# A two-layer graph network on one core: its front stage loaded, normalized, written and ranked in another way

## The reference, cut to what matters

```
x = x + gnn0(layernorm(x), edges, edge attributes)   # attention over incoming edges, 8 heads
x = x + ffn0(layernorm(x))                           # 64 slices per head
x = x + gnn1(layernorm(x), edges)
x = x + experts(layernorm(x))                        # top 2 of 8 experts
```

## Time and profile before

| what | value |
|---|---|
| median of 3 runs | 4086.47 us (4084.59 to 4089.71) |
| span of the profiled execution | 4086.3 us |
| front stage (`sort_nodes`) | 1.1 to 236.2 us |
| `windows` (edge records put into slots) | 237 to about 345 us |
| layer 0's graph loop | about 345 to 1560 us |
| the slice network | about 1560 to 2000 us |
| layer 1's graph loop | about 2000 to 2950 us |
| experts | about 2950 us to the end |

### The profile page before, as it was taken

How to read it: one execution, slowest core, us unless ns; L and a number is a source line. 1 busy time by engine, 2 the same in 40 slices (tenths; PEclk the granted TensorE clock), 3 DMA queues, 4 the chain that set the end, 5 groups by cost and what they waited for, 6 DMA issues and landing times. The chain is left out here.

```text
span 4086.3 us, 69498 instructions
## 1 busy us (share of the span) xinstructions
PE 2989.6 (73%) x12787; PEld 2168.3 (53%) x12788; DVE 2289.9 (56%) x5023; ACT 1298.0 (32%) x5485; POOL 2301.6 (56%) x2343
## 2 busy tenths in 40 slices
PE   4623777787878887999666665665656489999998
PEld 3422444444444444667544444444444378898887
DVE  4533888888888887874355555555555611111111
ACT  1401444444444454432211111111111533333343
POOL 5156777777777773002577777777777623333332
PEclk9866999899999998998777777778777789999999
DMA  8635444344444442000244444444444756666564
GB/s 188 193 89 147 116 116 117 105 108 108 108 107 109 110 111 62 0 2 30 75 112 113 113 112 113 112 113 113 113 112 112 220 173 166 170 174 167 167 172 128
DMA packets 292188, 487.96 MB, mean 119 GB/s; under 512 B 145315, under 2 KB 193393, under 8 KB 291625
## 3 DMA queue, kind: packets, MB, share of 16 engines
q0 software_dynamic: 127312, 325.41, 32.1%
q1 hardware_dynamic: 155936, 158.55, 13.2%
q10 hardware_dynamic: 8880, 3.34, 0.4%
HBM read 430.09 MB, written 57.50 MB: 119 GB/s over the span
## 5 line engine op out<-in xcount | busy, mean ns | idle before, releaser
L902 POOL DMA_INDIRECT g_rows<-rows,g_recs x1856 | 1764.1, 950 | 628.9 <-issue 474.1
L947 PE MATMUL g_pA<-g_msg,k_ident 128*128 128x264 f32 (+1 forms) x3712 | 1150.2, 463 | 474.0 <-DVE g_pA L1141 409.4
L947 PEld LDWEIGHTS g_pA<-g_msg,k_ident 128*128 128x128 f32 x3712 | 805.4, 228 | 803.8 <-issue 659.1
L936 PE MATMUL g_pE<-g_ew,g_recT 128*128 128x512 f32 x932 | 511.8, 676 | 251.3 <-DVEq L1125 248.4
L1135 DVE TENSOR_TENSOR g_msg<-g_rows,g_pp 128x1024 f32 (+3 forms) x464 | 571.9, 1233 | 151.2 <-DVEq L84 151.1
L1985 POOL DMA_INDIRECT out<-e_ys,e_goal x102 | 160.7, 1576 | 501.8 <-issue 481.1
L936 PEld LDWEIGHTS g_pE<-g_ew,g_recT 128*128 128x128 f32 x932 | 170.0, 202 | 468.9 <-DVEq L1125 343.1
L2038 PE MATMUL e_pY<-e_w,e_hT 128*128 x1632 | 373.8, 382 | 30.3 <-issue 30.3
L1057 ACT ACTIVATE g_pp<-g_dd 128x32 f32<-128x32 f32 x464 | 95.2, 205 | 921.0 <-ACTq L84 921.0
L2027 PEld LDWEIGHTS e_pH<-e_xT,e_w 128*128 128x128 f32 x3264 | 382.9, 193 | 5.2
L2027 PE MATMUL e_pH<-e_xT,e_w 128*128 128x128 f32 x3264 | 383.2, 276 | 0.0
(11 more groups left out here) (418 smaller groups left out, 3446.2 us busy)
## 6 DMA issues: line engine op xcount, KB each, us to landing
e_w<-in_L_ffn_W SPq DMA_DIRECT2D x110, 1024.0 KB
g_rows<-rows,g_recs POOLq DMA_INDIRECT x1856
g_recs<-slots SPq DMA_DIRECT2D x468, 8.0 KB
tok<-e_xall SPq DMA_DIRECT2D x7, 910.0 KB
rows<-p_row SPq DMA_DIRECT2D x50, 119.0 KB
own<-p_row SPq DMA_DIRECT2D x50, 119.0 KB
p_x<-in_x SPq DMA_DIRECT2D x1, 5600.0 KB
own<-p_x SPq DMA_DIRECT2D x1, 5600.0 KB
```

Source lines behind the costliest of these rows:

```text
L902: pool.indirect_dma_start(out=rows[:, r, j, :], out_offset=None, in_=rows_d, in_offset=bass.IndirectOffsetOnAxis(ap=recs[:, r, 4 * j:4 * j ...
L936: last = t_.matmul(pE[:, c:c + 512], recT[:], ew[:].rearrange("p c d -> p (c d)")[:, c:c + 512], start=True, stop=True)
L947: last = t_.matmul(sums, K["ident"][:], of, start=False, stop=(j == C - 1), skip_group_check=True)
```

## The change

Nothing is changed in what is computed; the order of nodes within the last bucket of the sort may differ. Six edits, all but the last in `sort_nodes`:

1. The weights `wn` and `wx` are loaded by SP's queue ahead of x, not by ACT's. x comes in five parts of ten tiles (10240 bytes a partition each), with a semaphore for each.
2. DVE's order is by part: block numbers of ten tiles, some counts (`marks`: 0, 2, 4, 6, 4), statistics and variance of the part (`piece`), and the factors of the part before (`scaled`). The waits for the weights and for POOL's constants, and two new casts (`tri_b`, `ones_b`), now stand ahead of the first block numbers. ACT takes three square roots ahead of tile 0 and two more ahead of tiles 1 and 5's work.
3. The counting matmuls write to three PSUM banks that the row pipeline doesn't use.
4. Rows are written once, to `own0` only, by pairs of tiles (RB=6 buffers, three pairs); x's columns follow after each ten tiles, the edge records after the pair of tiles 30 and 31. All loops over tiles are unrolled.
5. 32 buckets in place of 64 (degrees of 31 and more share the last one), the one-hot matrix and its two weights in bf16, 4 pieces of 16 tiles, which alternate between two pairs of PSUM banks. `ranks` now stands after tile 39 in PE's program.
6. Layer 0's graph loop gathers the same 272 columns from `own0`, whose rows lie 2112 bytes apart, in place of `rows0` with 1088.

```diff
+DB = 32
-        J, R, RB, W, GT, PG, B = 2, 10, 5, 10, 10, 5, 2
+        J, R, RB, GT, PG, B = 2, 10, 6, 10, 5, 2
-        OHW = NT * NB
+        OHW = NT * DB
+        NG = NT // GT
+        hot = m.sb("p_hot", [P, NT, DB], BF16)
+        banks = (pX, pTt, pR)
+        pN = [banks[g % 3][0:P, 16 * (g // 3):16 * (g // 3) + GT] for g in range(NG)]
+        sides = ((pR, pTt), (pM, pX))
-        cols = [(a, min(a + 8, NT)) for a in range(0, NT, 8)]
+        cols = [(a, min(a + 16, NT)) for a in range(0, NT, 16)]
 # SP
-                for l in lanes:
-                    sp.dma_start(x[l, :, :], ...).then_inc(x_in, 16)
+                sp.dma_start(wn[:], ...).then_inc(w_in, 16)
+                sp.dma_start(wx[:, :, 0:D], ...).then_inc(w_in, 16)
+                for g in range(NG):
+                    for l in lanes:
+                        sp.dma_start(x[l, g * GT:(g + 1) * GT, :], ...).then_inc(x_in[g], 16)
-                        for l in lanes:
-                            sp.dma_start(rows0[l, bass.ds(W * u + r, 1), :]..., row[l, r % RB, :]).then_inc(row_out[r % RB], 16)
-                            sp.dma_start(own0[l, bass.ds(W * u + r, 1), 0:RW]..., row[l, r % RB, :]).then_inc(row_out[r % RB], 16)
+                for t in range(0, NT, 2):
+                    sp.wait_ge(row_ok, t + 2)
+                    j = t // 2 % (RB // 2)
+                    for l in lanes:
+                        sp.dma_start(own0[l, t:t + 2, 0:RW], row[l, 2 * j:2 * j + 2, :]).then_inc(row_out[j], 16)
+                    if t % GT == GT - 2:
+                        g = t // GT
+                        sp.wait_ge(x_in[g], 32)
+                        for l in lanes:
+                            sp.dma_start(own0[l, g * GT:(g + 1) * GT, RW:RX], x[l, g * GT:(g + 1) * GT, :]).then_inc(x_out, 16)
+                    if t == 3 * GT:
+                        sp.wait_ge(rec_made, 2)
+                        ... # the edge records, both lanes
 # DVE
+                def piece(g):
+                    dve.wait_ge(x_in[g], 32)
+                    for t in range(g * GT, (g + 1) * GT):
+                        last = norm.tile(v, t, x[:, t:t + 1, :])
+                    last.then_inc(tile_ok, 1)
+                    dve.wait_ge(tile_ok, g + 1)
+                    norm.variance(v, ch, stats, slice(g * GT, (g + 1) * GT))
-                index(0)
                 dve.wait_ge(w_in, 64)
                 dve.wait_ge(consts, 3)
+                v.tensor_copy(tri_b[:], K["tri"][0:P, 0:P])
+                v.tensor_copy(ones_b[:], K["ones"][0:P, 0:P])
+                marks = (0, 0, 2, 6, 12, 16)
+                for g in range(NG):
+                    index(g)
+                    for t in range(marks[g], marks[g + 1]):
+                        count(t)
+                    piece(g)
+                    if g:
+                        scaled(g - 1)
 # ACT
+                for g in range(3):
+                    root(g)
+                normed(0)
+                for t in range(NT):
+                    if t in (1, 5):
+                        root(3 + t // 5)
 # PE
+                project(0, 40)
                 ranks()
-                group(3, False, False)
-                group(4, False, True)
+                project(40, NT)
 # graph
-    rows_d, xk = dr[f"rows{layer}"], K["x"]
+    rows_d, xk = dr["own0" if layer == 0 else "rows1"], K["x"]
```

More of the change, by code:

```diff
@@ L487, in turned @@
[L487 to L495, removed]
-                    s.activation(row[:, r % RB, :], pH[r % 2][:, 0:RW], ACT.Copy).then_inc(row_ok, 1)
@@ L498, in group @@
-                def group(u, first, last_group):
-                    for r in range(W):
-                        if r < W - 1 or not last_group:
-                            normed(u, r + 1)
-                        turned(u, r)
-                        if r > 0:
-                            rows(u, r - 1, first and r - 1 < RB)
-                    rows(u, W - 1, False)
-                normed(0, 0)
-                paired(act, NT // W, group)
+                for g in range(3):
+                    root(g)
@@ new lines, in normed, with turned, rows @@
+                def normed(t):
+                    if t % GT == 0:
+                        act.wait_ge(rst, t // GT + 1)
+                    s.activation(xn[:, t % 2, :], x[:, t, :], ACT.Identity, bias=nbias[:, t:t + 1], scale=rstd[:, t:t + 1]).then_inc(xn_ok, 1)
+                def turned(t):
+                    act.wait_ge(t_ok, t + 1)
+                    s.activation(xnT[:, t % 2, :, :], pT[t % 2][:, :, 0:P], ACT.Copy).then_inc(xnT_ok, 1)
+                def rows(t):
+                    act.wait_ge(h_ok, t + 1)
+                    if t >= RB:
+                        act.wait_ge(row_out[t % RB // 2], 32 * (t // RB))
+                    s.activation(row[:, t % RB, :], pH[t % 2][:, 0:RW], ACT.Copy).then_inc(row_ok, 1)
@@ L515, in _, with counting @@
                 pe.wait_ge(below_ok, J)
-                for t in range(NT):
-                    for j in range(J):
-                        last = t_.matmul(pN[t // GT][:, t % GT:t % GT + 1], bl[:, j, t, :], ones[:], start=(j == 0), stop=(j == J - 1))
-                    last.then_inc(counted, 1)
+                def counting(g):
+                    if g >= 3:
+                        pe.wait_ge(idx_ok, g - 2)
+                    for t in range(g * GT, (g + 1) * GT):
+                        for j in range(J):
+                            last = t_.matmul(pN[g][:, t % GT:t % GT + 1], bl[:, j, t, :], ones[:], start=(j == 0), stop=(j == J - 1))
+                        last.then_inc(counted, 1)
+                counting(0)
                 pe.wait_ge(ablk_ok, 1)
@@ L562, in place @@
                     last.then_inc(placed, 1)
+                for g in range(1, NG):
+                    counting(g)
                 pe.wait_ge(wx_ok, 1)
-                turn(0, 0)
-                group(0, True, False)
-                group(1, False, False)
-                group(2, False, False)
+                turn(0)
+                project(0, 40)
                 ranks()
-                group(3, False, False)
-                group(4, False, True)
+                project(40, NT)
                 for g in range(NT // PG):
```

144 lines of the change are left out of this document (64 added, 80 removed).

## The result

| | median, us | lowest to highest, runs |
|---|---|---|
| before, same chip | 4085.53 | 4081.34 to 4089.71, 4 |
| after | 4011.18 | 4008.13 to 4011.93, 4 |

The account below looks back on a forecast made before the run. The front stage (235 us) was taken as bound by a chain that changes engines. Terms -22, -1.7, +6, -17.6, -11.8 and -17 brought its end from 236.2 to 172.9, 63 us: 4086.3 - 63 = 4023, range 4004 to 4048.

Parts of the forecast that it names:

- fetches land early: Rival, chance 0.20: beside smaller x packets, front-stage fetches land in 10 us; 4012, or 4004 if PE is never late.
- No wait for the weights: Front, ahead of the first block numbers: the wait costs nothing if weights land by 17; first fetch stays near 19.7.
- I go nearer to the upper end: 46.: Front: fetch 5, issued at 27.3, lands at 46 us, within 32 to 52, beside the loads of x.
- The taking of turns: Each DMA engine takes packets from its queues in turn; a fetch beside x needs some 9 us.
- Counts, -22: Front, fetches and counts: fetch 16 goes at 51.5, then POOL is unbroken; last count done at 109.5, was 131.2.
- DMA engines bind more: Rival, chance 0.22: fetches and writes slow each other, fetches at 1.75 us, counts end at 117.5; 4034.
- PE at `ranks` at 124: Front, row pipeline: tile 0 at 51, DMA engines then ACT bind, PE reaches `ranks` at about 124; net +6 us.
- VectorE's wait for the first sum, 9: Front: DVE waits for TensorE's first sum of `ranks`, 115 to 124, some 9 us.
- Rounds 6.4, first pair 0.7: Front, rounds of `ranks`: three full and a small one at the copies' pitch, 6.4 us against 24.0, so -17.6.
- Passes halve, -11.8: Front, DVE's passes after the rounds: 24.5 us, all but 0.9 halves with 1600 elements, -11.8.
- Place, the wait of 17 goes, 29.8 to the end: Front's end: PE reaches `place` at 143, the 16.97 us wait goes (-17); DVE's groups end at 172.9.
- I am wrong if that loop moves by more than 10 us.: Sign against the prediction: layer 0's loop, expected still some 1215 us, moves by more than 10 us.

Follow-up runs that it names:

- e12: Changed kernel with the loads of x's parts 2 to 4 and the edge data held behind the first two counts: 4019.08 us, ratio 0.9829.
- e4: Changed kernel with x's columns written behind all rows, not after each ten tiles: 4008.09 us, ratio 0.9795.
- e7: Changed kernel with the statistics of four parts ahead of the counts on VectorE: 4001.94 us, ratio 0.9791.
- e11: Changed kernel with the reorderings of e7 and e4 together: 3998.76 us, ratio 0.9781.
- e3: Kernel before with only the 32 buckets in bf16 and two pairs of banks, `ranks` still after tile 29: 4070.49 us, ratio 0.9951.
- e8: Changed kernel with `ranks` after tile 29 in place of tile 39: 4015.34 us, ratio 0.9823.
- e2: Kernel before with only layer 0's gathers taken from the wide table `own0`: 4088.39 us, ratio 0.9997.
- e9: Kernel before with seven more semaphore increments in the front on VectorE alone: 4063.18 us, ratio 0.9937.
- e5: Kernel before with only the bucket cap set to 31, so node order changes but no instruction is added or removed: 4087.22 us, ratio 1.0001.

## Why the prediction was right, and where it was wrong

The kernel is faster by more than the forecast said and the time lies in the range, but two errors stand against each other in it: the front gave 15 us less than forecast, later stages 29 us that it did not have. That the time came within 12 us is luck. The time is that of the rival "fetches land early" (4012), whose steps did not happen: it had the last count at 101.6 and tile 0 at 43.

- *No wait for the weights.* VectorE waited 2.5 us, for a constant of POOL, and the first fetch was at 19.8 against 19.69. Right.
- *"I go nearer to the upper end: 46."* This step failed. Fetch 5 was there for its count at 55.3 to 55.9, not 46. I took the six fetches as landing together after one latency. They came one behind another: counts at 37.1, 44.0, 49.8, 52.3, 55.3, 55.9. e12 shows the cause, the loads beside them. The taking of turns, as the prediction worked it out (one packet of q1 for each of a fetch's ten on an engine), is too cheap by far: from 19 to 37 us q1's 458 packets took 92.1% of the engines' time, 0.58 us each, so ten turns would be 5.8 us, and even with the 5.9 of a fetch alone before them 11.7, not 17.4. For each of q0's 253 packets q1 got 1.8 through; why is open. Tile 0 followed at 61.5, not 51 (+10.5).
- *Counts, -22.* Measured -7: the last one was done at 124.2. 11.1 of the 14.7 us too few are the late start (fetch 16 issued at 62.65, not 51.5). 2.1 were lost among the 33 fetches behind it, in one wait for a count (1.58 at 79.00) and one issue of 2.12 us (at 83.52); the others kept the pitch of 1.51, so "fetches stay at 1.51 us" was right, and the 1.75 of the rival "DMA engines bind more" did not come. The last 1.5 are a later landing of fetch 49 (issued at 114.58). VectorE waited 3.75, 3.23, 3.60 and 3.42 us for fetches (at 96.7, 100.6, 116.2 and 120.3), 10 to 14 us after x's columns had been issued, but these waits held up no later fetch. In e4 and e7 the last count was late behind its fetch where a big write stood beside it, in e11 neither was so.
- *PE at `ranks` at 124.* Measured 139.07, +15.1: 10.5 from tile 0, 4.6 from 40 tiles that took 77.6 us and not 73. (The prediction's sum has a slip here: from tile 27 to 40 there are 13 tiles of 1.36 us, not ten, so that by its own steps ScalarE would end at 125.7 and not 121.6.) Nor does it name the square root of part 3 ahead of tile 1, for which ScalarE stood until 70.31. The reason that I gave, DMA engines full, is not what the windows show (0.80 busy from 100 to 130, against 0.99 in the earlier trace rows): ScalarE stood for single late writes, 6.15, 6.77 and 1.03 us, and in e4, by order alone, the longest ahead of `ranks` is 0.80.
- *VectorE's wait for the first sum, 9.* Measured 10.93. Both ends of it moved by 14 to 15 us, so that it came out nearly right.
- *Rounds 6.4, first pair 0.7.* 144.74 - 139.07 = 5.7, first pair 0.63. Right; the copies pitch at 1.55.
- *Passes halve, -11.8.* 24.5 became 157.96 - 144.74 = 13.2, so -11.3. Right. The multiply by the bf16 matrix took 1.83, the same as the subtraction in 32 bits beside it (148.26), so these mixed types do not run twice as fast. The tier table that the prediction cited ("VectorE: DVE Perf Modes", section "The perf-mode tier table", the Trainium skill) has the double rate of two-input operations for bf16 data and single for 32-bit ones, and no row for mixed; the trace agrees with the prediction's reading of it.
- *Place, the wait of 17 goes, 29.8 to the end.* 188.2 - 157.96 = 30.2. Right. In e3, where the rows are late, this wait grew to 46.4, and in e8 13.3 of it came back.
- *Sum 63.* Measured 48.0; the 15 missing are the 15.1 by which TensorE was late at `ranks`.
- *"I am wrong if that loop moves by more than 10 us."* It moved by 10.3, and not by the table (e2); a shift of VectorE's code alone does the same (e9). "Their instructions stay" was true and no reason for the time to stay. With the experts (13.1) it was worth 23.4; the other 5.8 of the 29.2 are in loop 1 and the stages between, where e5, with before's code, shows 5.1 of them too. Without the 29.2 the time would have been about 4040, 17 over the forecast and not 12 under it.

## What to carry to other kernels

Small fetches issued together beside a big load land one by one (counts at 37.1 to 55.9 us here), so cost each of them and keep what does not need them ahead of them in the program: e7's order of VectorE's work was worth 11 us for a table of six numbers. Halving work ahead of a wait gives nothing while the awaited part is late (e3); look for which side waits before and after each step. When an edit adds or removes instructions ahead of a hot loop, time the loop apart, and run a version that only shifts the code: here 7 increments were worth a third of what six edits were (25.3 of 74.3 us), and without such a run they would have been credited to the edits (e3's 17.7 us above all).

## What the runs showed of the hardware

Seven semaphore increments on VectorE ahead of the loops made a program of 4088 us take 4063. A turn of layer 0's loop over tiles has a wait of VectorE's own sequencer of 1.11 or 0.89 us, and the experts take 786 to 798 or 773 to 779 us, by VectorE's program ahead of them. Which places are good was not tried: only shifts of 7 and of the edits themselves were run. A fetch of 212.5 KB landed within 5.9 us with the loads held back (e12), and its count ran 17.4 us behind its issue beside them.
